# Layer 2 attention in row tiles: GpSimd alone norms the values, and ScalarE issues their transfers

## The reference

```
def _L2_xattn_ref(x, context, mask, ln1_s, ln1_b, lnc_s, lnc_b, Wq, Wkv, null_kv, Wo, lno_s, lno_b):
...
    xn = _ln(x, ln1_s, ln1_b)
    cn = _ln(context, lnc_s, lnc_b)
    q = xn @ Wq
    kv = cn @ Wkv
    k, v = jnp.split(kv, 2, axis=-1)
```

## Time and profile before

| What | Value |
| --- | --- |
| Median of three runs | 2301.94 us |
| The profiled execution | 2306.95 us, span of its core 2305.2 us |
| Layer 2 attention, from the first scores to the last weighing step | 895 to 1730 us |
| PE busy over the span | 2006.2 us (87%) |
| DVE, ACT, POOL busy over the span | 1470.6, 1351.8, 903.1 us |

### The profile page before, as it was taken

The page is one execution under the profiler, slowest core; times in us unless marked ns, Lnnn a source line. Parts: engine busy times, 40 slices in busy tenths (PEclk is TensorE's granted clock), DMA queues, the critical chain, the costliest instruction groups (busy, mean ns, idle before and its releaser), DMA issues. The chain is left out here.

```text
span 2305.2 us, 52296 instructions
## 1 busy us (share of the span) xinstructions
PE 2006.2 (87%) x21121; PEld 1412.6 (61%) x21121; DVE 1470.6 (64%) x2958; ACT 1351.8 (59%) x2425; POOL 903.1 (39%) x728
## 2 busy tenths in 40 slices
PE   6999999768997997788888878887867889999997
PEld 3777777557885454456565655655664447777774
DVE  5677778679984453656555555655623667777784
ACT  5778777536763223666656566656630367777763
POOL 6655654037771931324222233332120054344310
PEclk7999999779998999899999999999988989999997
DMA  6445544224522123343344433433210155444420
GB/s 169 140 136 155 140 142 125 66 66 127 147 80 57 37 70 104 100 124 105 101 127 111 113 101 107 121 100 100 72 45 10 52 147 148 134 131 137 135 77 9
DMA packets 105519, 240.03 MB, mean 104 GB/s; under 512 B 45688, under 2 KB 54928, under 8 KB 105024
## 3 DMA queue, kind: packets, MB, share of 16 engines
q1 hardware_dynamic: 105280, 236.69, 36.8%
HBM read 155.38 MB, written 0.65 MB: 68 GB/s over the span
## 5 line engine op out<-in xcount | busy, mean ns | idle before, releaser
L1655 PE MATMUL L2ps<-L2work,L2values 32*128 32x224 f32 x6144 | 346.8, 375 | 86.9 <-ACT L2values L1787 64.7
L1636 PE MATMUL L2ps<-L2keys,L2qz 128*128 128x384 f32 x896 | 347.9, 532 | 64.8 <-DVE L2negmax L1849 64.8
L1655 PEld LDWEIGHTS L2ps<-L2work,L2values 32*128 32x128 f32 x6144 | 308.0, 198 | 151.0 <-issue 119.6
L1866 DVE STREAM_TRANSPOSE L2work<-L2work 128x1568 f32<-128x1568 f32 x112 | 202.8, 1811 | 187.5 <-PE L2ps L1655 186.7
L1636 PEld LDWEIGHTS L2ps<-L2keys,L2qz 128*128 128x128 f32 x896 | 170.1, 200 | 205.5 <-DVE L2negmax L1849 72.5
L1781 ACT ACTIVATE L2work<-L2work,L2rinv 128x1536 f32<-128x1536 f32 x112 | 176.6, 1577 | 188.2 <-DVE L2rinv L1871 188.2
L1849 DVE CUSTOM_DVE_ANT_0 L2work<-L2ps,L2maskadd,L2big 128x1536 f32<-128x1536 f32 x112 | 203.3, 1815 | 70.4 <-PE L2ps L1636 65.0
L654 ACT ACTIVATE L3probsT<-L3ps 128x448 f32<-128x448 f32 x384 | 196.1, 547 | 70.5 <-PE L3ps L511 65.9
L654 ACT ACTIVATE L0probsT<-L0ps 128x448 f32<-128x448 f32 x384 | 198.3, 552 | 47.9 <-PE L0ps L511 46.8
L1776 ACT ACTIVATE L2work<-L2work,L2negmax 128x1536 f32<-128x1536 f32 x112 | 175.6, 1568 | 69.6 <-DVE L2negmax L1849 69.6
L1728 POOL COPY L2values<-L2null_column 128x12 f32<-128x12 f32 x64 | 13.2, 206 | 475.9 <-DMA L2values<-in_ctx 459.7
(11 more groups left out here) (484 smaller groups left out, 4061.2 us busy)
## 6 DMA issues: line engine op xcount, KB each, us to landing
L2values<-in_ctx SPq DMA_DIRECT2D x192, 192.0 KB, 6.2
L0key_stack<-L0key_parts SPq DMA_DIRECT2D x192, 187.5 KB
L3key_stack<-L3key_parts SPq DMA_DIRECT2D x192, 187.5 KB
L0ctxT<-in_ctxT SPq DMA_DIRECT2D x16, 750.0 KB, 4.3
L1rawT<-in_ctxT SPq DMA_DIRECT2D x16, 750.0 KB, 6.6
L2mean_spread<-L_moments SPq DMA_DIRECT2D x16, 750.0 KB, 7.3
L3ctxT<-in_ctxT SPq DMA_DIRECT2D x16, 750.0 KB, 4.5
L2wqk<-L_moments SPq DMA_DIRECT2D x15, 750.0 KB, 24.3
```

The costliest lines, as they stand in the source:

```text
L1636: last = nc.tensor.matmul(PS[:, score_bank(m) + w, 0:NCH * BW], tile_rows(m), key_window(b, w), start=True, stop=True)
L1655: last = nc.tensor.matmul(PS[:, 4 + a, 0:RT * BW], V[a * BW:(a + 1) * BW, n, :], block_cells(a, b, n), start=n == 0, stop=n == BLOCKS - 1, ...
L1866: nc.vector.transpose(turned_cells(b, t), SM[:, m % 2].rearrange("p (g r n) -> p g r n", g=RT, n=BW)).then_inc(s.turned, 1)
```

## The change

GpSimd norms all 12 blocks of each window; the parts of DVE and ACT go, with `values_due` and two of the three semaphores that PE waited for. The transfers of values move from SP's stream into ACT's, as four DMA instructions behind the scaling of certain tiles: window 0 of batch b in loop step 7b + 2, window 1 in 7b + 4, window 2 in 7b + 6, and window 3 in 7b + 7. The waits on `pv_done` move along. SP keeps all other transfers in their old order. On POOL, the norm of window 2 of a batch moves ahead of the norm of the next keys. The rest of the diff is line numbers.

```diff
-POOL_CHUNKS, DVE_CHUNKS, ACT_CHUNKS = range(5), range(5, 8), range(8, NCH)
...
             for b in range(1, B + 1):
                 ahead_of = b + 2 < B
                 if b + 1 < B:
                     load_keys(b + 1)
-                if b >= 2:
-                    load_values(b - 1, 2)
-                    load_values(b - 1, 3)
-                if b < B:
-                    load_values(b, 0)
                 if ahead_of:
                     load_moments(b + 2)
-                if b < B:
-                    load_values(b, 1)
                 if ahead_of:
                     load_mask(b + 2)
...
-                pe.wait_ge(s.v_pool, groups)
-                pe.wait_ge(s.v_act, groups)
-                pe.wait_ge(s.v_dve, groups)
+                pe.wait_ge(s.values_ready, groups)
...
-                for c in POOL_CHUNKS:
+                for c in range(NCH):
                     x = V[:, w * NCH + c, 0:P - 1]
                     last = nc.gpsimd.tensor_scalar(x, x, VST[:, 1, w, b, c:c + 1], VST[:, 0, w, b, c:c + 1], ALU.mult, ALU.add)
-                last.then_inc(s.v_pool, 1)
+                last.then_inc(s.values_ready, 1)
...
             for b in range(1, B + 1):
+                if b >= 2:
+                    normalise_values(b - 1, 2)
                 if b + 1 < B:
                     normalise_keys(b + 1)
                 if b >= 2:
-                    normalise_values(b - 1, 2)
                     normalise_values(b - 1, 3)
...
+            def load_values(b, w):
+                if b:
+                    last_step = (NCH * w + NCH - 1) // RT
+                    act.wait_ge(s.pv_done, RT * (b - 1) + last_step + 1)
+                else:
+                    act.wait_ge(s.v_zeroed, 1)
+                n = BW if w < WINDOWS - 1 else LAST_KEYS
+                for a in range(4):
+                    nc.scalar.dma_start(V[a * BW:a * BW + n, w * NCH:(w + 1) * NCH, :], src["ctx"][b][w * BW:w * BW + n]
+                                 ).then_inc(values_loaded[w], 16)
...
+            for w in range(WINDOWS):
+                load_values(0, w)
             act.wait_ge(s.constants, 1)
             mask(0)
             for n in range(TILES + LAG):
...
                 if n < TILES:
                     scale(n)
+                if t in (2, 4, 6) and 1 <= b < B:
+                    load_values(b, t // 2 - 1)
+                if t == 0 and 1 <= b - 1 < B:
+                    load_values(b - 1, 3)
                 if t == (2 if b == 0 else 5) and b + 1 < B:
                     mask(b + 1)
-                if n == 0:
-                    act.wait_ge(s.offsets_ready, 1)
-                for v in values_due(n):
-                    normalise_values(*v)
...
-            def normalise_values(b, w):
-                dve.wait_ge(values_loaded[w], 64 * (b + 1))
-                for c in DVE_CHUNKS:
...
-                for v in values_due(n):
-                    normalise_values(*v)
```

More of the change, by code:

```diff
@@ L1486, in attention_16_wide_heads @@
                        "values_loaded0 values_loaded1 values_loaded2 values_loaded3 mask_loaded null_rows null_column constants margins mask_ready "
-                       "v_zeroed stats_zeroed stats_spread offsets_ready v_pool v_act v_dve moments_filled moments_ready moments_stored slot_ready keys_loaded0 keys_loaded1 spread_loaded keys_moved keys_scaled "
+                       "v_zeroed stats_zeroed stats_spread offsets_ready values_ready moments_filled moments_ready moments_stored slot_ready keys_loaded0 keys_loaded1 spread_loaded keys_moved keys_scaled "
                        "scores_filled max_done exp_done rinv_ready scaled turned pv_done heads_ready out_filled out_ready dve_chain")
@@ L1536, in block_cells @@
             return of.rearrange("p (t r g n) -> p t r g n", t=RT, r=RT, g=RT)[:, :, r, g]
[L1538 to L1542, removed]
         def step_blocks(g):
@@ L1550, in _ @@
         def _(sp):
[L1551 to L1560, removed]
             def load_mask(b):
@@ L1596, in _ @@
                         sp.dma_start(VST[a * BW:a * BW + n, x, w], of[w * BW:w * BW + n]).then_inc(s.stats_spread, 16)
-            load_values(0, 0)
+            sp.wait_ge(s.v_zeroed, 1)
             for a in range(4):
@@ L1600, in _ @@
                 sp.dma_start(V[at:at + 1, BLOCKS - 1, :], k.ident[P - 1:P, :]).then_inc(s.null_rows, 16)
-            load_values(0, 1)
             load_keys(1)
-            load_values(0, 2)
-            load_values(0, 3)
             load_moments(1)
@@ L1852, in maximum @@
                                                ALU.add, ALU.min, nmax[:, m % 4:m % 4 + 1]).then_inc(s.max_done, 1)
-            def normalise_values(b, w):
-                dve.wait_ge(values_loaded[w], 64 * (b + 1))
-                for c in DVE_CHUNKS:
-                    x = V[:, w * NCH + c, 0:P - 1]
-                    last = nc.vector.tensor_scalar(x, x, VST[:, 1, w, b, c:c + 1], VST[:, 0, w, b, c:c + 1], ALU.mult, ALU.add)
-                last.then_inc(s.v_dve, 1)
             def turn(m):
```

## The result

The changed kernel takes 2398.1 us, the median of four runs, against 2302.52 us of the kernel before: a ratio of 1.0413, with a 95% interval of 1.0389 to 1.0438.

What follows compares the result with a forecast made beforehand. The prediction took the loop through window 3 (issue, landing, norm, weighing; 51.2 us a batch) as the bound. Terms of +133, +13, +5 and -9 made +142 on 2301.94: 2444 us, range 2360 to 2510.

Steps and rivals of the forecast that it cites:

- Issue behind a scaling: Window 3's issue on ACT waits for copies and a scaling after the last weighing step: +3.8 us a batch, no range.
- Longer norm and slow clock: From landing to end of weighing: POOL norms 12 blocks, then PE runs at a 0.50 clock: +1.0 us a batch.
- Moments on the same engine: Moments, now in another queue, get in ahead of window 3's end on its one DMA engine: +4.5 us a batch.
- Mask and keys before the landing: Mask and next keys now come before window 3 lands: 0 to 3.5 us a batch, taken as +1.8.
- The sharing: Moments' 16 packets go ahead on window 3's engine: 3.6 to 5.7 us, taken as +4.5; rival without sharing, chance 0.11.
- The covers: PE's wait for window 3, some 20 us, hides removed norms and ACT's issues: 0; uncovered, issues cost up to 5 us.
- the rival that made the norms the limit: PE works through 39.4 us a batch once DVE's and ACT's norms go: 2125 us, chance 0.02.
- The start: Before the first weighing: moments come early, but ACT issues 16 transfers ahead of the first mask: -9 us, or 0.
- The last three batches: Batches 13 and 14, without moments, masks or keys behind them, together +13.4 us; batch 15, without scaling, +4.5 us.
- The rival with the other sign: Window 3 in its own queue, not stretched by bursts, lands sooner: 2.3 us less a batch, 2276 us, chance 0.06.
- Its turning point: The result turns faster when window 3 lands less than 30.7 us after its issue (51.2 - 3.8 - 16.7).

Runs made afterwards that it cites:

- e8: Changed kernel, with SyncE's mask and next keys alone waiting until window 3 has landed, moments as in the changed kernel: 2371.55 us, ratio 1.0277.
- e1: Kernel before, with GpSimd norming all 12 blocks and SyncE still issuing every transfer in the old order: 2315.88 us, ratio 1.0053.
- e6: Changed kernel, with each 29-row transfer of window 3 cut into one of 16 and one of 13 rows: 2119.46 us, ratio 0.9203.
- e7: Kernel before, with GpSimd norming all 12 blocks, SyncE issuing in the old order, and window 3 cut into 16 and 13 rows: 2118.0 us, ratio 0.9194.
- e9: Changed kernel, with ScalarE's issue of window 3 ahead of its copies, and moments, mask and keys waiting for window 3's landing: 2260.83 us, ratio 0.9787.
- e3: Changed kernel, with ScalarE's issue of window 3 moved ahead of its copies of the weighed sums: 2348.32 us, ratio 1.0190.
- e4: Changed kernel, with SyncE's moments, and the mask and keys after them, waiting until window 3 has landed: 2307.9 us, ratio 1.0026.

## Why the prediction was right

The mechanism held: the period of a batch is the way through window 3, what the change removes lies beside it, and what it lengthens lies on it. One link was wrong, when ACT's transfers start. Three of the four terms were too large, and so the forecast stood 46 us too high, within a range 150 us wide. The sizes of the terms, as predicted and as measured per batch:

| Term | Predicted | Measured | From |
| --- | --- | --- | --- |
| Issue behind a scaling | 3.8 | 1.97 | 2.03 - 0.06 |
| Longer norm and slow clock | 1.0 | 0.57 | 15.78 - 15.21 |
| Moments on the same engine | 4.5 | 3.3 | e8 - e1 |
| Mask and keys before the landing | 1.8 | 2.3 | changed - e8 |
| The window itself | 0 | -0.8 | e1 - before, landing |
| Sum | 11.1 | 7.3 | 58.53 - 51.22 |

**The issue** was the term most off, and the only one that I gave no range. I took ACT's transfers to start when the scaling ahead of them ends. In the trace they start with it, both at 1266.16, and so in batches 1 to 14: they wait for `pv_done` alone, and ACT hands them on while it still computes. 12 x 1.83 = 22 of the 46 us lie here.

**The sharing** came at 3.3, a little under my lower bound of 3.6, which was the price of the 16 packets one behind another. That the moments get in is plain from the page of the changed kernel, where the second of them lands after 16.3 us instead of 24.3, 11.7 us ahead of window 3 on the mean:

```profile
L2mean_spread<-L_moments SPq DMA_DIRECT2D x16, 750.0 KB, 8.6
L2wqk<-L_moments SPq DMA_DIRECT2D x15, 750.0 KB, 16.3
```

The Trainium skill, "DMA: Bandwidth & Descriptors", section "Queues, rings and completion order", has an engine go round between its queues; the traces agree in that the second moments transfer lands before window 3, and window 3 pays for it. One reading was wrong without harm. Both transfers count on one semaphore, so the first's 7.3 us is the 16th of 32 counts and not its landing: in the kernel before the last two counts come at 1279.58 and 1281.39, both behind window 3.

**Mask and keys** cost 2.3 for 1.8. On the mean the mask lands 1.1 us ahead of window 3 and the keys 2.5 us behind it, so only a part of them counts, as assumed.

**The norm and the clock.** Landing to PE took 5.6 us for 5.9, and the first step after the wait 4.8 us on the mean instead of 5.4. In the batch shown it took 4.39, at a mean granted clock of 0.65; in the last batch of the kernel before it was 0.50.

```profile
1254.40:1258.70 4.30, 4.28 (x56) 0.65 0.00 0
```

**The covers.** The norms taken off DVE and ACT were worth nothing, as said, and 85 us where window 3 is out of the way; the time is then what the rival that made the norms the limit gave (2125; e6 and e7 ended at 2119 and 2118). ACT's time for its transfers is real: the next exponential starts at 1269.96, 0.10 us after the last of the four ends, and DVE's maximum for it was there at 1268.83. But PE has no pause there. In e6 against e7 it costs nothing that can be measured even without cover, where I had allowed up to 5 us a batch.

**The start** gave -10.3 for -9, by the way described: the 16 transfers take ACT 14.3 us, and DVE begins the first tile at 906.5. The last three batches gave +13 for +18.

The rival with the other sign, a window 3 of its own queue that bursts no longer stretch, fell: bursts stretch it as before, and the second queue adds sharing. Its turning point, a landing less than 30.7 us after the issue, was worked out with an issue 3.8 us late; in e9, where window 3 is issued at once, 32.8 us is enough. Why the window lands 0.8 us sooner in e1 than before, in the same queue and order, stays open; window 1 is issued 22.9 us after T there instead of 29.3, and in batches 13 and 14 the window lands later than before, 33.0 and 33.4 us after its issue instead of 31.5 and 31.2.

## What to carry to other kernels

Before counting what an edit takes off the engines, follow the longest wait back to its transfer and see whether it closes a loop; what lay beside that loop here was worth nothing until the loop was shortened, and 85 us then. A transfer that runs on one DMA engine is the first thing to look for, here by 24 to 30 GB/s in the transfers' row while PE waits; cut into 16 and 13 rows, it turned a loss of 96 us into a gain of 185. And moving a transfer into another queue also frees those that used to stand behind it: here they ran into it, for 3.3 us a batch.

## What the runs showed of the hardware

- ACT's transfer instructions can start while the computing instruction ahead of them still runs: both at 1266.16, the scaling 1.60 us long. In e3 and e9 they start 0.55 us into an exponential of 1.57 us.
- The fourth transfer of 29 rows is held up on ACT as on SP: it takes 1.97 to 3.87 us in batches 1 to 14 of the changed kernel, and 2.45 to 5.67 before (but 0.31 in one batch); the first three take at most 0.33. What stands behind it on ACT waits. In e3 these are the copies, 2.64 us in this batch, and PE's next weighing step starts 0.10 us after them:

```profile
1245.96 2.73 ACTq L1762 DMA_DIRECT2D L2values<-in_ctx  x1
1248.73 1.09 ACT L1768 COPY L2qz<-L2ps 128x224 f32<-128x224 f32 x4 [2.64 <-issue]
1249.92 2.93 PE L1625 MATMUL L2ps<-L2work,L2values 32*128 32x224 f32 x56 [2.18 <-issue]
```

- Two queues share one DMA engine: in the changed kernel the last of the moments' 32 counts comes at 1295.30, with window 3 of the other queue under way from 1266.16 to 1306.53. In one queue, before, the last two came 3.6 and 5.4 us after window 3's landing at 1276.0.
- A burst on the other engines slows a transfer on one, even where its packets on that one come later: 35.18 us with the moments' burst (e1) against 33.23 without (e4).
